# Four fused cross-attention layers on one core: where the third layer's MLP does its first norms, its function table and its sums

## The reference, cut to what matters

```
out = softmax(q k^T * scale + mask) v            # 16 heads of 16
hidden = out @ cproj_w + cproj_b + x             # the third layer's attention, residual
y = layer_norm(hidden, ln2_w, ln2_b)             # over 256 elements of a token
y = gelu(y @ fc_w + fc_b, approximate=True)      # 256 -> 1024
x = hidden + y @ proj_w + proj_b                 # 1024 -> 256
```

## Time and profile before

| | us |
|---|---|
| median of 3 runs (1018.63 to 1023.31) | 1018.9 |
| the profiled execution | 1019.49 |
| its span | 1017.7 |
| PE busy | 965.1 (95%) |
| DVE busy | 728.2 (72%) |
| ACT busy | 575.1 (57%) |
| POOL busy | 412.0 (40%) |

### The profile page before, as it was taken

How to read it: one execution, slowest core, us unless ns; L and a number is a source line. 1 busy time by engine, 2 the same in 40 slices (tenths; PEclk the granted TensorE clock), 3 DMA queues, 4 the chain that set the end, 5 groups by cost and what they waited for, 6 DMA issues and landing times.

```text
span 1017.7 us, 20133 instructions
## 1 busy us (share of the span) xinstructions
PE 965.1 (95%) x8028; PEld 824.6 (81%) x8028; DVE 728.2 (72%) x1261; ACT 575.1 (57%) x1193; POOL 412.0 (40%) x462
## 2 busy tenths in 40 slices
PE   7999999998889799999999999999999999988997
PEld 5667566555666699998899999999999999878997
DVE  4658899898678668854777666886667766776542
ACT  3456888787676544454554544455445554456442
POOL 3444589898886334310221223232222122264110
PEclk9999999999999999999999999999999999999999
DMA  9302000000000240024322334322221221200000
GB/s 304 97 1 84 1 2 1 1 1 1 2 1 1 58 172 1 1 84 146 104 76 72 103 116 132 120 91 84 84 78 55 77 84 42 84 2 11 22 21 32
DMA packets 31266, 62.30 MB, mean 61 GB/s; under 512 B 4419, under 2 KB 9285, under 8 KB 30533
## 3 DMA queue, kind: packets, MB, share of 16 engines
q1 hardware_dynamic: 31172, 61.02, 18.2%
HBM read 58.91 MB, written 2.10 MB: 60 GB/s over the span
## 4 chain that ended last, share of the span: by engine, by line
PE 73%; POOL 11%; DVE 7%; issue 4%; ACT 4%; DMA 0%; SPq 0%; POOLq 0%; DVEq 0%
PE work L916 11%; PE work L773 6%; PE work L775 6%; PE work L774 6%; PE work L1029 6%; PE scores L773 5%; PE scores L775 5%; PE scores L774 5%; PE work L993 5%; POOL pair L2152 3%; PE work L1011 2%; PE work L700 2%; PE work L635 2%; POOL pair L2155 2%; PE work L533 2%
## 5 line engine op out<-in xcount | busy, mean ns | idle before, releaser
L2108 POOL TENSOR_SCALAR stat<-stat 128x2 f32<-128x2 f32 (+2 forms) x50 | 11.6, 233 | 284.3 <-DVE stat L1163 282.8
L1575 DVE TENSOR_REDUCE smax<-scores 128x16 f32<-128x1024 f32 x32 | 39.2, 1225 | 111.4 <-PE scores L775 111.4
L916 PE MATMUL work<-ctxT,w 128*128 128x128 f32 x960 | 112.6, 275 | 0.2 <-DVE all_values L1560 0.2
L916 PEld LDWEIGHTS work<-ctxT,w 128*128 128x128 f32 x960 | 109.9, 192 | 0.8 <-issue 0.8
L2267 POOL TENSOR_TENSOR probs<-probs,smax 128x1024 f32<-128x1024 f32 x22 | 41.9, 1903 | 120.8 <-DVE smax L1600 120.8
L1977 ACT ACTIVATE all_keys<-work 128x512 fp32r<-128x512 f32 x64 | 38.2, 598 | 76.2 <-PE work L993 76.2
L773 PE MATMUL work<-all_values,pT_l_high 128*128 128x256 f32 x256 | 75.0, 293 | 3.5 <-DVE pT_l_low L1568 3.5
L773 PE MATMUL scores<-all_keys,src_l_high 128*128 128x256 f32 x256 | 74.1, 290 | 0.0
L775 PE MATMUL work<-all_values,pT_l_low 128*128 128x256 f32 x256 | 71.7, 280 | 0.0
L775 PE MATMUL scores<-all_keys,src_l_low 128*128 128x256 f32 x256 | 71.7, 280 | 0.0
L774 PE MATMUL work<-all_values,pT_l_high 128*128 128x256 f32 x256 | 71.7, 280 | 0.0
(11 more groups left out here) (212 smaller groups left out, 3084.9 us busy)
## 6 DMA issues: line engine op xcount, KB each, us to landing
w<-in_l_wk SPq DMA_DIRECT2D x32, 512.0 KB, 4.1
w<-in_l_wv SPq DMA_DIRECT2D x32, 512.0 KB, 5.0
w<-in_l_wq SPq DMA_DIRECT2D x8, 512.0 KB, 5.7
w<-in_l_wo SPq DMA_DIRECT2D x8, 512.0 KB, 6.0
x<-in_x SPq DMA_DIRECT2D x1, 2048.0 KB, 14.6
pair<-in_l_wo SPq DMA_DIRECT2D x4, 512.0 KB, 3.6
out<-x SPq DMA_DIRECT2D x8, 256.0 KB, 2.1
pair<-in_xT SPq DMA_DIRECT2D x1, 1536.0 KB, 8.9
```

The costliest lines, as they stand in the source:

```text
L916: last = mm(bank[:, h * P:(h + 1) * P], w[:, c, h * K3:(h + 1) * K3], ctxT[:, c, p * P:(p + 1) * P], start=(c == 0), stop=(c == DC - 1))
L1575: v.tensor_reduce(m, s3, X, ALU.max).then_inc(d_lmax, 1)
```

## The change

Six edits around turn 24 (`u == NU`):

1. The low part of the weights' piece 5 (`mlp_weight_low(5)`, `NU - 19` = 5) leaves turn 23's end on DVE and goes into turn 24.
2. In turn 24 `tile_sums` and `unit_reciprocals` of unit 23 go ahead of `unit_residual(22)`.
3. `mlp_stats(2)` goes from the loop over the batches (there behind `mlp_hidden_low(0, 2)`) into turn 24, before piece 5 and `unit_normal(23)`, and `mlp_norm(2)` behind `unit_normal(23)`, ahead of `mlp_affine(1)`.
4. `rstd(("m2", 2))` on POOL goes ahead of `mlp_bias(0)` and `mlp_bias(1)`.
5. The load of gelu's table on ACT goes from the loop's end into turn 24, behind the last `reciprocals_out`.
6. On ACT `mlp_weight_high(7)` goes ahead of `mlp_source_high(1)`.

No instruction is added or taken away. The norm of batch 3 and later ones stay where they were (batch 3's in the loop's turn `b = 1`). PE's and SyncE's streams are unchanged.

```diff
@@ vector, the loop over u @@
+                if u == NU:
+
+                    tile_sums(late[0])
+                    unit_reciprocals(u - 1)
                 if u >= 2:
                     unit_residual(u - 2)
...
-                if late:
+                if late and u < NU:
                     tile_sums(late[0])
...
-                if 0 < u <= NU:
+                if 0 < u < NU:
                     unit_reciprocals(u - 1)
+                if u == NU:
+                    mlp_stats(2)
+                    mlp_weight_low(NU - 19)
...
                 if 0 < u <= NU:
                     unit_normal(u - 1)
                 if u == NU:
+                    mlp_norm(2)
                     mlp_affine(1)
                     mlp_source_low(1)
...
                 for q in mlp_pieces(u - 1):
-                    mlp_weight_low(q)
+                    if u != NU - 1:
+                        mlp_weight_low(q)
@@ vector, the loop over b @@
-                if b + 2 < B:
+                if 0 < b < B - 2:
                     mlp_stats(b + 2)
                     mlp_norm(b + 2)
@@ scalar @@
                 if u == NU:
+
+                    act(scratch[:, :], tanh_gate[:, :], ACT.Gelu_apprx_tanh)
+                    for q in mlp_pieces(u):
+                        mlp_weight_high(q)
                     mlp_source_high(1)
...
                 for q in mlp_pieces(u):
-                    mlp_weight_high(q)
+                    if u < NU:
+                        mlp_weight_high(q)
...
-            act(scratch[:, :], tanh_gate[:, :], ACT.Gelu_apprx_tanh)
             for b in range(B):
@@ gpsimd, the loop over u @@
+                if u == NU:
+                    rstd(("m2", 2), TT)
...
             for b in range(2, B):
-                rstd(("m2", b), TT)
+                if b > 2:
+                    rstd(("m2", b), TT)
                 mlp_bias(b)
```

## The result

| | before | after |
|---|---|---|
| median of 7 and 7 runs, us | 1021.65 | 1015.94 |
| lowest to highest | 1018.63 to 1023.84 | 1013.48 to 1016.99 |
| profiled execution, span | 1019.49, 1017.7 | 1013.48, 1011.7 |
| mean granted clock of the profiled execution | 0.993 | 0.997 |

The ratio is 0.9942, 95% interval 0.9928 to 0.9957: 5.9 us faster (4.4 to 7.4; the two medians are 5.7 apart), where 6.6 were forecast. The forecast time of 1012.3 us and its range to 1015.2 were missed, by 3.6 and 0.7 us: with four more runs of the kernel before, its median is 1021.65 and not 1018.9.

The account below looks back on a forecast made before the run. PE, busy 95% of the span, was taken as the bound, its idle or slow time as the gain. 1.0 (sums) + 3.98 (stall) + 1.58 (clock) = 6.6 us gave 1012.3 us, between 1011 and 1013.8; all likely cases 1009.8 to 1015.2.

Parts of the forecast that it names:

- the last of the sum: From the profiled execution's 1019.49 less 6.6 to 1012.9, then 0.6 lower for the median: 1012.3 us.
- C: Rival: the second stall, 1.76 us at 412, no longer lowers the clock; 1.5 us more gained, 1010.8; chance 0.09.
- The sums earlier: Last unit's sums on DVE start sooner, so PE's reciprocal transposes come 1.0 us earlier; bounds 0 and 1.6.
- The norm: Batch 2's statistics, root and norm done earlier on DVE and POOL, so PE's wait before batch 2's source goes.
- the stall of 3.98 us: PE's idle time between hidden(1,1) and mlp_source(2), waiting for DVE's norm; forecast to go wholly.
- The meeting with POOL's additions: DVE's norm beside POOL's two bias additions: one addition, 1.3 us, taken; bounds 0 and both, 2.5; hidden from PE.
- The table: Gelu's table load in ACT's idle time: first gelu at about 347.5 instead of 349.67, so projected(0) need not wait.
- The clock: The lower clock after PE's long stall belongs to that idle time and should not come: 1.58 us gained.
- B: Rival: a shorter stall remains, projected(0) waits 0.7 to 1 us, the clock falls anyway; 4.1 us gained, 1014.8; chance 0.17.
- D: Rival: DVE and POOL set the pace in later batches, PE's wait grows by 6.6 us; 1018.9 stays; chance 0.04.
- E: Rival: the lower clock belongs to the loads, not the stall, so the kernel is slower, 1020.3; chance 0.04.

Follow-up runs that it names:

- e4: Kernel before with 32 matmuls that nobody reads in PE's idle time ahead of batch 2's norm; 1019.08 against 1022.65 us, ratio 0.9971.
- e3: Kernel before with only the last unit's sums and reciprocals moved ahead of the residual and of weights' piece 5; ratio 0.9999.
- e6: Changed kernel with POOL's bias additions of batches 0 and 1 behind that of batch 2; 1014.38 us.
- e1: Kernel before with only batch 2's statistics, root and norm moved earlier; 1017.9 against 1022.65 us, ratio 0.995.
- e5: Changed kernel once more, beside the kernel before on another chip; 1015.53 against 1022.48 us, ratio 0.9931.
- e9: Changed kernel with the residual and last low part ahead of the query weights' sums in each batch; 1009.8 against 1021.25 us, ratio 0.9882.
- e7: Changed kernel with the query weights' addition, in MLP batches 3 to 5, between batch b + 2's statistics and its norm; 1012.21 us.

## Why the prediction missed, point by point

**The step that failed is the last of the sum**, "the median is 0.6 below that execution, so 1012.3 us". Three runs (1023.31, 1018.9, 1018.63) were taken as the kernel's level. The 50 runs beside the experiments have a median of 1022.5 and reach from 1017.88 to 1027.79, and they follow the mean granted clock. Two of the three were low for this kernel. Why is not shown, since their clocks are not on record; the profiled execution, 1019.49 at 0.993, lies 2 us under the line of e4, and one of its falls, at 413 us, cost nothing (C below). With 1021.65 in its place the same sum gives 1015.05, 0.9 us from the measured time. A range for a time, and not for a difference, should have held this spread; mine reached 2.9 us up. The gain itself was nearly right (6.6 against 5.9), but partly by chance, as the following points show.

**The sums earlier:** 1.0 us forecast; 1.03 measured in PE's start of L716 (4.02 to 2.99 us behind L700; 4.02 to 2.98 in the changed kernel). Alone it brought nothing (e3), because the stall behind it stayed and its lower clock lasted longer; at equal clock the gain is there.

**The norm:** the stall of 3.98 us went wholly, as forecast. The meeting with POOL's additions cost 2.52 - 0.73 = 1.8 us, between the one addition taken and both. Both met it: taken singly, the norm's two instructions run from 342.87 to 344.11 and from 344.03 to 345.39, and the additions from 342.67 to 343.96 and from 343.92 to 345.24. Each instruction of the norm started within 0.2 us behind an addition and ended 0.15 us behind it. That agrees with the rule quoted from the Trainium skill. PE's slack hid it (e6). The affine began at 345.31, 7.75 us behind L700; forecast 345.8, 7.5 behind.

**The table:** needed, as forecast. The first gelu came at 346.87, 9.31 us behind L700, forecast 9.2. Without it (e1) `projected(0)` waits, about 0.7 us where I had 1.5, and the stretch is 2.40 us longer than with all edits: 1.02 of it the sums', 0.71 this wait, 0.67 the wait of `hidden(1,0)` for the first gelu, which I had at nothing.

**The clock:** the cause was right. e4 shows it apart from everything else: PE busy, the same loads, no fall. It also answers the rule of the Trainium skill on the clock's gate: the trace agrees. The fall at 413 us is not the only other one, as the prediction has it: the profile before has two more, at 28 us and at 263, and the latter too stands behind idle time, without loads:

```profile
260.00:262.00 2.00, 0.04 (x1) 0.00 (x0) 1.84 (x6) 1.02 (x2) 1.04 (x2) 1.00 0.00 0
...
264.00:266.00 2.00, 2.00 (x19) 0.73 (x18) 1.64 (x5) 1.57 (x3) 1.83 (x4) 0.50 0.00 0
```

The size was that of one execution, and taken against batch 3's 7.58 us; against the changed kernel's own 7.68 it is 1.48. Over 11 runs the filler is worth 3.0 us (1.7 to 4.3), and in e3 the lower clock costs 2.59. If all of the 3.0 belongs to this stall, an estimate of the gain is 1.0 + 3.98 + 3.0 = 8.0 us on average; measured are 5.9 (4.4 to 7.4) and, in e5, 7.1 (5.4 to 8.6). Whether the first is chance or the changed kernel has lower clocks elsewhere more often (its mean is 0.9933, the filler's 0.9954) stays open. In the changed kernel's two profiles (here and e5) the falls lie at 28, 259, 419 and 1001 us and later, in different executions at different places.

**The rivals.** B (a shorter stall, clock down) did not happen. D (given back later) is out: from `hidden(1,3)` to the first value product it is 463.78 - 366.72 = 97.06 us before and 456.24 - 359.18 = 97.06 after. E (the loads lower the clock) is out by e4 and the windows above. C had a false price. The fall at 413 us, 0.59 in 413 to 415 and 0.55 in 415 to 417, was gone in the changed kernel's profile, but that stage took the same 97.06 us. In the kernel before, the next stall of PE is shorter by what the lower clock cost, 0.30 us and not the 1.77 of the changed kernel:

```profile
425.87 0.36 PE L773 MATMUL work<-m_w_high,m_hid_high 128*128 128x256 f32 x1 [0.30 <-issue]
```

```profile
418.32 0.36 PE L773 MATMUL work<-m_w_high,m_hid_high 128*128 128x256 f32 x1 [1.77 <-issue]
```

So in these profiles the lower clock is free there only while a stall is still to come that it can fill. In e5 and e6 it fell behind the last of the three stalls, and the same stage took 457.98 - 359.44 = 98.54 and 457.29 - 358.78 = 98.51 us, 1.5 more. In e5's profile:

```profile
420.00:422.00 2.00, 2.00 (x12) 2.00 (x11) 1.27 (x2) 1.95 (x4) 0.00 (x0) 0.50 0.00 0
```

This may be a part of what is open above; how often it happens in runs without a profile is not shown.

## What to carry to other kernels

Forecast the difference, and take the level of the time from many runs with the granted clock beside each, since a stall of a few us on TensorE costs its own length and then a stretch at the lower clock whose length varies. Where PE waits behind an engine that has more than one errand in a loop, put what PE waits for ahead of what only the next stage needs: that move (e9) was worth 5.6 us in this stage, where the change studied had brought 6.8 in its own. Look first at what runs on GpSimd beside it, since here the old place lost 1.78 us to such a neighbour. And a free place in one engine's wait is free only if the engine waited for is not slowed by what is put there, as POOL's root was in e7.

## What was not expected of the hardware

- 32 matmuls that nobody reads, put into a wait of 3.8 us, made the kernel faster, 1019.08 against 1022.65 us.
- The time fell with the mean granted clock by 0.84 us for each 0.001, with 0.56 us left over (the line in e4).
- A 128x2 instruction of POOL took 1.10 us instead of 0.23 beside DVE's 128x1024 addition of two SBUF operands (e7), DVE's two norm instructions 2.52 us instead of 0.73 beside POOL's two additions, and a 128x512 low part on DVE 2.47 us instead of 0.69 beside POOL's 128x1024 product.
- The lower level of the clock can begin before PE has work again (0.85 in 354 to 356 us in e3, with PE idle until 356.60).
- A stretch at the lower clock cost 1.5 us or nothing in the stage behind `hidden(1,3)`, by whether PE had another stall still ahead (e5 and e6 against the kernel before).
